# A cross-attention turn on one Trainium2 core, with the pieces of TensorE's turn, V's copies and the maxima in another order

## What is computed

```python
q = split_heads(layernorm(x) @ Wq.T + bq)
k = split_heads(ctx @ Wk.T + bk)
v = split_heads(ctx @ Wv.T + bv)
scores = einsum('bhqd,bhkd->bhqk', q, k) / sqrt(16)
scores = where(mask == 0, -1e9, scores)
p = softmax(scores, axis=-1)
x = x + (einsum('bhqk,bhkd->bhqd', p, v) merged) @ Wo.T + bo
x = x + moe(layernorm(x))      # router, the top 2 of 8 experts, w1, silu, w2
```

## Time and profile before

| | |
|---|---|
| median of 3 runs | 584.5 us (583.47 to 586.1) |
| the profiled execution's own time | 583.73 us |
| its span, first to last instruction | 582.0 us |
| TensorE matmuls busy | 434.5 us, 75% |
| TensorE weight loads busy | 383.9 us, 66% |
| VectorE busy | 375.2 us, 64% |
| ScalarE busy | 231.3 us, 40% |
| GpSimd busy | 263.9 us, 45% |
| attention turns | from about 68 to 310 us |
| mean granted clock of TensorE | 0.873 of 2.4 GHz |

### The profile page before, as it was taken

The page is one execution under the profiler, slowest core; times in us unless marked ns, Lnnn a source line. Parts: engine busy times, 40 slices in busy tenths (PEclk is TensorE's granted clock), DMA queues, the critical chain, the costliest instruction groups (busy, mean ns, idle before and its releaser), DMA issues.

```text
span 582.0 us, 10906 instructions
## 1 busy us (share of the span) xinstructions
PE 434.5 (75%) x4123; PEld 383.9 (66%) x4123; DVE 375.2 (64%) x733; ACT 231.3 (40%) x296; POOL 263.9 (45%) x170
## 2 busy tenths in 40 slices
PE   3557799999999999999987472005999999998000
PEld 2445588888888888888767462004999999998000
DVE  3765657777777777777735855001999999996233
ACT  3321235555555555555561130002545545553000
POOL 7352412222222222222006003774798999895574
PEclk9787769999999999999998685556999999999655
DMA  8979499999999999997245502426678878862354
GB/s 187 188 187 243 166 146 124 145 144 144 146 143 147 146 143 147 144 148 104 34 129 179 201 1 82 170 99 193 192 232 260 239 250 246 241 214 91 108 155 133
DMA packets 82504, 93.00 MB, mean 160 GB/s; under 512 B 19824, under 2 KB 75280, under 8 KB 82464
## 3 DMA queue, kind: packets, MB, share of 16 engines
q1 hardware_dynamic: 74064, 79.61, 64.6%
q0 software_dynamic: 2688, 7.34, 3.9%
q10 hardware_dynamic: 5712, 5.51, 2.8%
HBM read 51.58 MB, written 22.14 MB: 127 GB/s over the span
## 4 chain that ended last, share of the span: by engine, by line
PE 46%; issue 21%; DVE 14%; ACT 8%; POOL 5%; DMA 3%; ACTq 2%; SPq 1%; DVEq 0%; POOLq 0%
PE ps L1178 17%; PE ps L1228 10%; PE ps L1243 7%; PE ps L1257 7%; POOL chosen_rows L614 4%; ACT h_hi L775 3%; ACT h_f L774 2%; DVE y_out L1112 2%; DVE k_f L827 2%; ACTq L779 1%; DVE neg_max L843 1%; PE ps L1270 1%; DVE h_lo L1105 1%; DVE x_rows_sb L890 1%; PE ps L1399 1%
## 5 line engine op out<-in xcount | busy, mean ns | idle before, releaser
L843 DVE TENSOR_REDUCE neg_max<-ps 112x1 f32<-112x376 f32 x256 | 132.8, 545 | 48.7 <-PE ps L1228 44.8
L592 POOL TENSOR_TENSOR w_lo<-w_raw,w_hi 128x1024 fp32r<-128x1024 f32 x42 | 117.8, 2824 | 24.1 <-DVE w_hi L1101 14.3
L664 ACT ACTIVATE probs<-ps 125x1344 f32<-125x1344 f32 x64 | 82.7, 1292 | 59.2 <-PE ps L1243 56.4
L1228 PE MATMUL ps<-k_stack,q_stack 98*112 98x376 f32 x256 | 90.8, 396 | 10.5 <-issue 5.7
L502 POOL TENSOR_TENSOR k_lo<-k_f,k_hi 128x752 fp32r<-128x752 f32 x16 | 28.7, 1792 | 83.0 <-ACT k_hi L638 80.5
L493 POOL TENSOR_TENSOR ctx_lo<-ctx_raw,ctx_hi 128x752 fp32r<-128x752 f32 x16 | 28.8, 1799 | 79.2 <-ACT ctx_hi L631 79.2
L1228 PEld LDWEIGHTS ps<-k_stack,q_stack 98*112 98x112 f32 x256 | 42.9, 183 | 28.6 <-DVE neg_max L843 21.0
L1105 DVE TENSOR_TENSOR h_lo<-h_f,h_hi 128x1024 fp32r<-128x1024 f32 x21 | 52.6, 2503 | 11.1 <-ACT h_hi L775 11.1
L1243 PE MATMUL ps<-q_stack,k_stack 100*125 100x224 f32 x384 | 54.8, 279 | 2.1 <-ACT probs L664 1.3
L1243 PEld LDWEIGHTS ps<-q_stack,k_stack 100*125 100x125 f32 x384 | 51.2, 193 | 2.8 <-ACT probs L664 1.8
L1178 PE MATMUL ps<-flat_t_hi,w_hi 128*128 128x256 f32 x168 | 50.4, 300 | 3.4 <-DVE flat_t_lo L1094 3.1
(11 more groups left out here) (168 smaller groups left out, 986.0 us busy)
## 6 DMA issues: line engine op xcount, KB each, us to landing
w_raw<-w SPq DMA_DIRECT2D x42, 512.0 KB, 3.9
k_stack<-k_hi SPq DMA_DIRECT2D x64, 188.0 KB, 6.3
k_stack<-k_lo SPq DMA_DIRECT2D x32, 188.0 KB, 9.0
ctx_raw<-ctx_t SPq DMA_DIRECT2D x32, 187.5 KB, 9.1
q_stack<-q_scratch SPq DMA_DIRECT2D x32, 168.0 KB
sorted_x<-zeros SPq DMA_DIRECT2D x1, 5376.0 KB, 17.5
rows<-sorted_x SPq DMA_DIRECT2D x21, 256.0 KB, 4.0
sorted_y<-y_out ACTq DMA_DIRECT2D x21, 256.0 KB, 3.0
```

The lines of the kernel that those rows point to most:

```text
L592: pool.tensor_tensor(low[t.par][:, :, :], raw[:, :, :], high[t.par][:, :, :].bitcast(F32), ALU.subtract).then_inc(done, 1)
L664: act.activation(pf[j % 2][:, :, :], ps[0:CT, BK_ST:BK_ST + KT, 0:4 * S], ACT.Exp).then_inc(pf_ready, 1)
L843: dve.tensor_reduce(neg_max[:, s:s + 1], ps[0:S, BK_MAX + s % 2, 0:CP], AX.X, ALU.max, negate=True).then_inc(max_read, 1)
L1228: pe.matmul(ps[0:S, BK_MAX + a, 0:CP], qs[b.ring][0:R_MAX, q, S * a:S * (a + 1)], ks[b.ring][0:R_MAX, q, :], start=True, stop=True).then_i ...
```

## The change

On TensorE the 16 heads no longer stand in pairs but singly between the other pieces, except the last three. The three chunks of V come first, then the two output groups of the earlier batch. Each key tile is made in two halves of three matmuls (`parts`, by half of the contraction), which stand among the heads; the accumulation stays open between the halves. The turn ends with attn_transpose, the last half, and s3. The new turn in the short form: h0 v0 h1 v1 h2 v2 h3 o'2 h4 o'3 h5 s0 h6 out_transpose h7 K0a h8 K0b h9 s1 h10 o0 h11 K1a h12 s2 h13 h14 h15 o1 max_transpose attn_transpose K1b s3.

On ScalarE both copies of V, ctx_high and out_copy now stand ahead of exps(b, 0) and exps(b, 1). On VectorE `normalise` stands after the tenth maximum instead of the sixteenth.

```diff
--- before.py
+++ after.py
@@ -722,18 +722,16 @@
                 after, before = b.after(1), b.after(-1)
                 if has(b.after(2)) and b.n:
                     key_high(b.after(2))
-                if has(b):
-                    exps(b, 0)
                 if has(after):
                     values(after, False)
+                    values(after, True)
+                if has(b.after(3)):
+                    ctx_high(b.after(3))
                 if has(before):
                     out_copy(before)
                 if has(b):
+                    exps(b, 0)
                     exps(b, 1)
-                if has(after):
-                    values(after, True)
-                if has(b.after(3)):
-                    ctx_high(b.after(3))
                 if has(b):
                     exps(b, 2)
                 if has(before):
@@ -942,10 +940,11 @@
             def turn(b):
                 after, before = b.after(1), b.after(-1)
                 if has(after):
-                    maxima(after, range(H))
+                    maxima(after, range(10))
                 if has(before):
                     normalise(before)
                 if has(after):
+                    maxima(after, range(10, H))
                     max_rows(after)
                 if has(b.after(3)):
                     keys(b.after(3), 0)
@@ -1172,14 +1171,14 @@
 
         @block.tensor
         def _(pe):
-            def product(o, terms):
+            def product(o, terms, first=True, final=True):
 
                 for n, (lhs, rhs) in enumerate(terms):
-                    last = pe.matmul(o, lhs, rhs, start=n == 0, stop=n == len(terms) - 1)
+                    last = pe.matmul(o, lhs, rhs, start=first and n == 0, stop=final and n == len(terms) - 1)
                 return last
 
-            def project_keys(b, t):
-                if t == 0:
+            def project_keys(b, t, parts=(0, 1)):
+                if t == 0 and 0 in parts:
                     pe.wait_ge(ch_ready, b.n + 1)
                     pe.wait_ge(cl_ready, b.n + 1)
 
@@ -1188,12 +1187,15 @@
                             pe.wait_ge(*{1: (vx_ready, 2), 2: (kf_ready, 4), 3: (vx_ready, 4)}[b.n])
                     else:
                         pe.wait_ge(vx_ready, 2 * (b.n - 1))
-                elif not early(b, 4):
+                elif 0 in parts and not early(b, 4):
                     pe.wait_ge(an_ready, b.n - 3)
                 m = slice(t * P, (t + 1) * P)
-                product(ps[:, BK_KV + t, 0:CP],
-                        [(w[:, 0, k, m], c[b.par][:, k, :]) for k in range(KD)
-                         for w, c in ((wh, ch), (wl, ch), (wh, cl))]).then_inc(kproj_done, 1)
+                for k in parts:
+                    last = product(ps[:, BK_KV + t, 0:CP],
+                                   [(w[:, 0, k, m], c[b.par][:, k, :]) for w, c in ((wh, ch), (wl, ch), (wh, cl))],
+                                   first=k == 0, final=k == KD - 1)
+                if KD - 1 in parts:
+                    last.then_inc(kproj_done, 1)
 
             def project_values(b, k3):
 
@@ -1298,38 +1300,45 @@
                     if has(after):
                         project_values(after, k3)
 
-                heads(0, 1)
+                def keys(t, part):
+                    if has(b.after(3)):
+                        project_keys(b.after(3), t, (part,))
+
+                heads(0)
                 values(0)
+                heads(1)
+                values(1)
                 heads(2)
+                values(2)
+                heads(3)
                 outputs(before, 2)
-                heads(3, 4)
+                heads(4)
+                outputs(before, 3)
+                heads(5)
                 scores(0)
-                heads(5)
-                values(1)
                 heads(6)
-                outputs(before, 3)
-                heads(7, 8)
+                if has(before):
+                    out_transpose(before)
+                heads(7)
+                keys(0, 0)
+                heads(8)
+                keys(0, 1)
+                heads(9)
                 scores(1)
-                heads(9)
-                values(2)
                 heads(10)
                 outputs(b, 0)
-                heads(11, 12)
+                heads(11)
+                keys(1, 0)
+                heads(12)
                 scores(2)
-                heads(13)
-                if has(before):
-                    out_transpose(before)
-                heads(14, 15)
+                heads(13, 14, 15)
                 outputs(b, 1)
                 if has(after):
                     max_transpose(after)
-                if has(b.after(3)):
-                    project_keys(b.after(3), 0)
                 if has(before):
                     attn_transpose(before)
+                keys(1, 1)
                 scores(3)
-                if has(b.after(3)):
-                    project_keys(b.after(3), 1)
 
             first = Batch(0, 0)
 
```

## The result

The changed kernel takes 621.25 us (619.71 to 622.56, four runs) against 584.18 us (583.47 to 586.1) on the same chip; the ratio is 1.063 (95% interval 1.060 to 1.066). The forecast was 614.5 us, with 603 to 626 as its range.

What follows compares the result with a forecast made beforehand. It took TensorE to bound the kernel (13.85 us of pieces, 1.15 of waits a turn), with just-in-time transfers beside it. Twelve turns at 2.5 us plus 1 added 31 to 583.7: 614.7, said as 614.5, range 603 to 626.

Steps and rivals of the forecast that it cites:

- The turn: One attention turn on TensorE, pieces laid end to end with new waits: 17.5 us, 2.5 more than before.
- the seam: Turn's end to the next first value matmul: TensorE waits 0.95 us for VectorE's key copy, against 0.63 before.
- ScalarE's chain: V copies held by the fourth output group, then ctx_high and out_copy: out_t's transpose on TensorE waits 1.2 us.
- rival 2: Chance 0.07: ScalarE's and GpSimd's work is covered, only turn-end and last-head waits count; 15.6 us a turn, 590 to 592.
- GpSimd's ctx_lo: Made on GpSimd in 1.80 us after ctx_high, it holds the first half key tile on TensorE: 0.8 us wait.
- The tail: Heads 13 to 15 in a row, head 15 waiting for VectorE's maximum: 0.65 to 0.7 us, against 0.37 before.
- The transfers: Key stack by DMA lands 16.1 us after the turn's end; hidden with 1.4 us to spare at 17.5.
- Rival 1: Chance 0.05: the order works, 14.5 us a turn, but transfers limit it to 15.0 to 15.3; 583 to 588 us.
- The sum: Whole kernel: turns 1 to 12 add 30 us, turn 13 adds 1, turn 0 and expert stage nothing; 31 us.
- the clock: TensorE's granted clock, expected to stay at 2.4 GHz despite more waits; costed at nothing.
- The third rival: Chance 0.05: TensorE falls to 1.2 GHz in part of the turns; one in four gives about 645 us.

Runs made afterwards that it cites:

- mended orders: Kernel before with s3 moved last, 590.62 us; changed kernel with third V buffer, earlier second key copy and a later half key tile, 589.96 us.
- key copy first: Changed kernel with VectorE copying the second key tile ahead of attn_low: 612.02 us, ratio to the kernel before 1.049.
- cut transfers: Second pair of key transfers cut to an eighth, scores wrong: kernel before with s3 last 575.99 us; changed kernel with three mends 582.23 us.
- out_copy first: Changed kernel with ScalarE's out_copy ahead of the two V copies, ctx_high still last of the four: 630.95 us, ratio to the kernel before 1.084.
- ctx_high first: Changed kernel with ScalarE making ctx_high ahead of the two V copies: 597.25 us, ratio to the kernel before 1.023.
- all mends: Changed kernel with third V buffer, second key copy ahead of attn_low, half key tile moved from behind head 11 to behind head 13: 589.96 us, ratio 1.010.
- quad last: Kernel before with the second key tile made ahead of the last score quad, so s3 ends the turn: 590.62 us, ratio 1.010.
- all mends with cut transfers: Changed kernel with third V buffer, earlier second key copy, later half key tile, and second key transfer pair cut to an eighth: 582.23 us, ratio 0.997.

## Why the prediction held, point by point

- *The turn.* Forecast 17.5, measured 17.49 in nine of twelve full turns. The method, laying the pieces end to end with start-to-start times, gave it, where the busy share of 97% would have hidden 1.15 us of waits a turn. That it agrees to a hundredth is in part luck. Counted from the first value matmul at 196.65, out_t's transpose is drawn from 6.83 us (forecast 6.8), the key tile from 8.30 (8.2) and the maxima's transpose from 15.06 (14.9); the seam behind it took 2.43 instead of 2.65. Three slips of the working move nothing: the terms of ScalarE's chain add up to 6.6 and not 6.7, while the key tile hangs on ctx_high's end at 6.15; h15 without a wait would stand at 13.1 and not 13.2, while it hangs on the maxima; and rival 2's turn is 15.5 by its terms, not 15.6.
- *ScalarE's chain.* Forecast 1.2 us, measured 1.2. The V copy is held by the fourth output group: the third V buffer, which takes away only that, brings some 26 us.
- *GpSimd's ctx_lo.* Forecast 0.8, measured 0.9 in the table. The claim that its cover was gone is borne out by both moves of ctx_high: two copies earlier ends the wait, one copy later makes it 2.0.
- *The tail.* Forecast 0.65 to 0.7; the largest wait for a maximum is 0.7. Moving the half tile was only run together with two other mends, so its own part wasn't measured apart.
- *The seam.* Forecast 0.95, measured 0.9, and 0.4 with VectorE's order swapped, where 0.45 was said.
- *The transfers.* Forecast as hidden with 1.4 us to spare at 17.5 us. No head waits for its key stack in the changed kernel: the last of the six transfers behind the turn's end at 195.6 is issued at 202.0 and lands 9.2 us later, at 211.3, 1.8 us before the turn ends at 213.1. Rival 1's limit, 15.0 to 15.3 a turn for a TensorE turn of 14.5, is what the runs with mended orders meet (15.3).
- *The sum.* From head 0 of the third turn's heads (87.9 before, 87.1 after) to that of the last (282.0 and 316.9) the changed kernel takes 35.75 us more. Twelve turns by 2.48 are 29.8, turn 13 is 14.87 instead of 13.97, 0.9. That is the 31 of the forecast, and it leaves 5.0.
- *What was mis-sized: the clock.* I costed it at nothing and gave its fall 5%. It fell in three of the twelve turns, for 3.4 us at a time (in the first of them twice, at 86.8 and 97.1), and these turns take 18.99, 18.98 and 19.53 us, 1.5, 1.5 and 2.0 too many: the missing 5 us. Two stretches inside the longer turns:

```profile
151.60:155.10 3.50, 3.50 (x21) 3.17 (x23) 1.93 (x5) 0.56 (x1) 0.00 (x0) 0.51 1.09 128
223.30:226.80 3.50, 3.50 (x32) 3.17 (x34) 2.24 (x5) 1.00 (x1) 0.00 (x0) 0.51 1.10 118
```

  The row that I had argued from, 7.71 of 12.00 us busy at 1.00, was no bound: less idling in another pattern did lower the clock. It also ended 0.9 us too early. The kernel before itself falls to 1.2 GHz at 310.9, just behind waits of 0.81 and 1.39 us, as it does at 72.0, 0.7 us after a wait of 1.67 us has ended:

```profile
72.10:82.10 10.00, 9.57 (x57) 8.18 (x57) 4.53 (x9) 4.26 (x5) 1.94 (x2) 0.50 0.98 133
298.00:310.90 12.90, 7.95 (x145) 5.91 (x137) 2.89 (x37) 7.02 (x10) 0.32 (x2) 1.00 0.38 126
310.90:314.30 3.40, 3.40 (x18) 3.40 (x18) 1.31 (x21) 0.00 (x0) 3.33 (x8) 0.50 0.52 174
```

```profile
71.32 1.72 PE L1228 MATMUL ps<-k_stack,q_stack 98*112 98x376 f32 x3 [1.67 <-DVE neg_max L843]
308.87 0.41 PE L1278 MATMUL ps<-ident,attn_rows 112*128 112x112 f32 x2 [0.81 <-DVE attn_rows L866]
310.67 0.36 PE L1178 MATMUL ps<-attn_w_hi,attn_t_hi 128*128 128x256 f32 x1 [1.39 <-DVE attn_t_lo L834]
```

  So the trace of the kernel before did hold falls behind waits of that size, and the clock deserved more than 5% and a term in the sum. The third rival came true in a quarter of the turns, though at 1.5 us a turn and not the 10 that I had priced it at, since TensorE stays at 1.2 GHz for a few us only. That the time is still within the range is luck in part: the range was made from the bounds of the waits, and they came out as forecast. The section "Part 1: The HAM clock gate" of the Trainium skill's page "TensorE: Matmul & The Clock Gate" says that activity releases the throttle, which speaks against an order with more idling. The trace agrees so far as the turns of the kernel before at 97% drawn busy show no fall and three of the changed kernel's twelve do; the kernel with the key copy first, which idles nearly as much, shows none.
- The rest of the 37.8 us: the start of the turns is 0.85 us earlier, the last turns add 1.4, and the stage of the experts, which the change doesn't touch, takes 1.5 us longer in this execution (272.9 from GpSimd's first fill to the end, 271.4 before). That goes with the clock too: in that stage it is at 1.2 GHz for 118.7 us instead of 112.7. Over the twelve profiled kernels, three have 118 to 119 us of it there and take 272.4 to 272.9; the nine others have 109 to 113 and take 271.0 to 271.5. For the 1.4 us no cause was looked for.

## What to carry to other kernels

Before a step is moved forward in an in-order engine's queue, look for the buffer that it writes and who reads it last: the step may start no earlier, and everything queued behind it then starts late, here two copies and, through them, GpSimd and TensorE. When two waits stand one behind the other, moving work to shorten the first can lengthen the second by more. And ask what lies just under the bound that is being removed: here the DMA engines at 97% left the mended order at 15.3 us a turn, where it takes 14.75 with cut transfers.

## What the runs showed of the hardware that was not expected

TensorE's granted clock fell from 2.4 to 1.2 GHz for 3.4 us at a time, in the changed kernel at 97.1, 151.7 and 223.3 us and in the kernel with out_copy first at 98.1, 118.6, 156.1, 193.6, 248.3 and 285.8. In each case that was 10 to 11.3 us after head 0, just behind the two waits at out_t and at the key tile (1.2 and 0.9 us, or 0.6 and 2.0). From 100 us to the turn without key tiles, the profiles of the kernels without that pair of waits, ctx_high first, third V buffer and all mends, show no fall. But the kernel with the key copy first has the pair too and shows none in the profiled execution, and the one with the quad last shows one, at 210.9, after a head had waited 1.9 us for its key stack. Near the start of the third turn of heads, at 86 to 88 us, four kernels show one: the changed one, ctx_high first, out_copy first, and all mends with cut transfers. So such waits go with the falls, while what decides whether one comes stays open.
